# Adaptive layer norm block: the context of global attention is transposed by DMA instead of TensorE, and the last batch's norm is spread over twelve tiles

## Chip, cores and metric

One core of a Trainium2 chip. The metric is the device time of one launch in microseconds. The kernel before takes 2309.56 us in the median of 3 runs (2308.02 to 2310.95).

## What is computed

```python
mod = (silu(c) @ wmod).reshape(4, 6, 1, 256)             # sa, ca, ga, sb, cb, gb
h = layernorm(x) * (1 + ca) + sa                         # x: 4 batches, 1024 tokens, 256
q, k, v = (heads(tanh(h @ W + bias)) for W, bias in ...) # 16 heads of 64
ctx = softmax(causal(q @ k.T / 8)) @ v                   # global attention, each batch
x = x + ga * tanh(merge(ctx) @ Wo + bo)
h = layernorm(x) * (1 + cb) + sb
for l in range(2):                                       # local attention and gated feed-forward
    h = layer(h)
x = x + gb * h
```

Products are made in about full precision: each operand is split into a high part and a rest (low part), and three products are summed (high by high, high by low, low by high).

## The kernel before, in words

**Phase 1** (`phase_modulation_and_attention`, up to about 967 us of the trace) treats the 4 batches in order, and in each batch 8 pairs of heads. Each engine runs its own instruction list; semaphores order them. In a list written out by hand, a pair's work is interleaved with the projections (V, Q, K; six of 128x512, L777) of the next pair. The scores of a pair come in 12 units (`UNITS`): units 0 to 3 belong to the first half of the queries (c = 0, 512 tokens), units 4 to 11 to the second half (c = 1). Units 8 to 11 cross the diagonal and have 1024, 768, 512 and 256 elements. For a unit TensorE makes the scores into one of two PSUM tiles (`score_products`, L799; it needs the exponentials of two units before), ScalarE the exponentials (`exps`, L621), VectorE the high and low part (`high_probs`, `low_probs`, L359 and L365), and TensorE the products with the values (`value_products`, L821) into `ps_o`. Tokens are then on the partitions.

The **context** is a half's result. VectorE takes reciprocals of the sums (L373) and multiplies (`normalise`, L380) into the f32 tile `ctx_tok`, 128x512. For c = 0 this is done in the middle of the pair, for c = 1 at its end. But both halves are transposed at the end: `context` (L841) makes four TensorE transposes of 128x128 through `ctx_tok` for each half, before and after unit 0 of the next pair's scores. (With `ctx_tok` as one buffer and c = 1 written after L847 of c = 0, the first group's transposes read the half normalised in mid pair.) ScalarE copies the PSUM result into `cT_hi` (L641), VectorE subtracts it from PSUM into `cT_lo` (L386). Both are f32r, with head channels on the partitions, for all 8 pairs and 1024 tokens. At the end of a pair's VectorE list also stand the low part of the next weights (`split_weights`, L349), for which TensorE's next projections wait, and that of the last projection (L357).

At a **batch's end** TensorE makes the output projection (L957 to L967): for each half c and each 128 output columns m, 8 pairs by three products of 128x512 from `cT_hi` and `cT_lo`. ScalarE takes tanh (L742), VectorE multiplies by ga (`gate_attended`, L561), TensorE transposes back (`output_T`, L856), VectorE adds (L571). Other work is hung in between: for batches 0 and 1 the norm and transposed input of batch b + 2, for batches 2 and 3 the second norm of finished batches: `second_statistics`, `second_normal` on ScalarE (L666, 8 instructions a batch, after the first tanh), `second_scale` and `second_offset` on VectorE (L440, L446). For batch 3, ScalarE also copies the first layer's weights (L749) and VectorE takes their low part (L605). In these lists an instruction that waits holds back everything behind it.

SyncE's list issues the DMAs: weights of the pair after next (`load_w`, L234), the transposing DMAs for the values (`transpose_values`, L240 and L242; inputs are [64, 1024] and [128, 1024], two bytes an element), inputs and results of batches.

**Phase 2** (`phase_layers`) has two layers of 32 tiles of 128 tokens (local attention) and 8 chunks (feed-forward). Tiles are written out for the first four (`V_RING`) and the last ones, and looped between. The last batch's second norm is done in the first four tiles of layer 1: after tile 0 VectorE makes 8 statistics (L1514) and the variance, after tile 1 the shifts (L1522) while ScalarE makes 8 normalising instructions (L1494), after tile 2 VectorE scales (L1526), after tile 3 it adds the offset (L1531). At a layer's start GpSimd makes inverse norms of keys (L1210) and queries (L1206), and then adds the rotated halves of the queries and the keys (`add_rotated`, L1214), whose sum TensorE transposes (L1890).

## Time and profile before

| | us |
|---|---|
| median of 3 runs | 2309.56 |
| the profiled execution's own time | 2310.14 |
| span of the profile, first to last instruction | 2307.8 |
| first pair to end of global attention | about 57 to 967 |
| layers 1 and 2 | about 969 to 2308 |

The profile is one execution. A timeline line gives start, duration, engine, line and operation, the output tile before the arrow and its inputs behind it. Runs of equal instructions are merged (x4), and then start and duration hold for all of them. Durations of neighbours on one engine overlap by 0.03 to 0.4 us, since they are pipelined; the distance of starts is what an instruction costs its engine. Idle time stands in brackets with what ended it.

### The profile page before, as it was taken

The numbers are of one execution on the slowest core, as the hardware profiler recorded it, in microseconds if no ns is written. First come the engines' busy times: TensorE is split into PE (matmuls) and PEld (weight loads), VectorE is DVE, ScalarE is ACT, GpSimd is POOL, SyncE is SP. The second block draws the span as 40 slices with busy tenths as digits, with TensorE's granted clock in tenths as the row PEclk, the third lists the DMA queues.
The fourth block names the chain that finished last, engine by engine and source line by source line (L and its number), as shares of the span: only waits on it lengthen the run. The fifth ranks groups of instructions, "written<-read, shape, count | busy, mean of one in ns | idle before, by whom it ended". The sixth has DMA issues, their size and how long they took to land.

```text
span 2307.8 us, 60013 instructions
## 1 busy us (share of the span) xinstructions
PE 2219.3 (96%) x20608; PEld 1701.0 (74%) x20608; DVE 1900.7 (82%) x4480; ACT 1481.4 (64%) x2937; POOL 526.4 (23%) x637
## 2 busy tenths in 40 slices
PE   6999999999999999789999998999999999998999
PEld 4676767676767666667777776788777777776888
DVE  6999799979998999678888887567588888886776
ACT  5777577757776777366767766444567767765343
POOL 2000000000000000244554554012355555551000
PEclk9999999999999999999999999999999999999999
DMA  4311231113121212300000001000100000001110
GB/s 134 68 32 39 58 56 32 39 53 61 32 69 49 53 32 44 124 1 2 9 0 9 0 9 49 10 0 0 49 1 4 6 4 5 5 4 32 61 36 28
DMA packets 135595, 74.98 MB, mean 32 GB/s; under 512 B 72645, under 2 KB 132925, under 8 KB 135233
## 3 DMA queue, kind: packets, MB, share of 16 engines
q1 hardware_dynamic: 135488, 73.60, 13.0%
q8 instruction: 63, 1.03, 0.2%
q14 instruction: 44, 0.35, 0.1%
HBM read 44.21 MB, written 8.40 MB: 23 GB/s over the span
## 4 chain that ended last, share of the span: by engine, by line
PE 53%; DVE 2%; issue 1%; ACT 1%; POOL 0%; DVEq 0%; POOLq 0%; ACTq 0%
PE ly_ps L75 9%; PE ly_ps L76 9%; PE ly_ps L77 9%; PE ly_ps L1919 6%; PE ly_ps L1898 5%; PE ly_ps L1909 5%; PE ly_ps L1936 5%; PE ly_ps L1890 3%; PE ly_ps L1929 1%; PE ly_ps L1946 1%; PE ly_ps L1974 1%; PE ly_ps L1867 1%; DVE ly_masked L1587 1%; ACT ly_probs L1360 0%; DVE ly_rope_t L1558 0%
## 5 line engine op out<-in xcount | busy, mean ns | idle before, releaser
L625 ACT ACTIVATE at_p<-at_ps_s,at_shift 128x1024 f32<-128x1024 f32 (+3 forms) x384 | 335.9, 900 | 70.2 <-PE at_ps_s L817 39.0
L368 DVE TENSOR_TENSOR at_p_lo<-at_p,at_p_hi 128x1024 f16<-128x1024 f32 (+3 forms) x384 | 358.6, 954 | 5.5
L1360 ACT ACTIVATE ly_probs<-ly_masked,ly_small,ly_rq 128x256 f32<-128x256 f32 x512 | 301.7, 594 | 13.9 <-DVE ly_small L1590 13.9
L836 PEld LDWEIGHTS at_ps_o<-at_v,at_p_hi 128*128 128x128 f16 x2304 | 208.5, 97 | 58.2 <-issue 38.8
L836 PE MATMUL at_ps_o<-at_v,at_p_hi 128*128 128x65 f16 x2304 | 237.8, 195 | 6.0 <-DVE at_p_lo L368 3.1
L1214 POOL TENSOR_TENSOR ly_rope_a<-ly_rope_a,ly_rope_t 128x512 f32<-128x512 f32 x128 | 164.2, 1283 | 315.6 <-DVE ly_rope_t L1558 315.6
L837 PE MATMUL at_ps_o<-at_v,at_p_hi 128*128 128x64 f16 x2304 | 236.1, 193 | 0.0
L838 PE MATMUL at_ps_o<-at_v,at_p_lo 128*128 128x65 f16 x2304 | 234.9, 193 | 0.0
L1587 DVE CUSTOM_DVE_ANT_0 ly_masked<-ly_ps,ly_mask 128x256 f32<-128x256 f32 x512 | 195.8, 419 | 46.7 <-PE ly_ps L1898 35.7
L363 DVE CAST at_p_hi<-at_p 128x1024 f16<-128x1024 f32 (+3 forms) x384 | 206.4, 555 | 19.3 <-ACT at_p L625 15.4
L1368 ACT ACTIVATE ly_operands_plain<-ly_ps 128x512 f32<-128x512 f32 x256 | 153.2, 599 | 107.6 <-PE ly_ps L1909 99.7
L838 PEld LDWEIGHTS at_ps_o<-at_v,at_p_lo 128*128 128x128 f16 x2304 | 211.6, 98 | 0.0
L837 PEld LDWEIGHTS at_ps_o<-at_v,at_p_hi 128*128 128x128 f16 x2304 | 211.4, 99 | 0.0
L631 ACT ACTIVATE at_stage<-at_ps_m,at_bias 128x512 f32<-128x512 f32 x192 | 131.6, 686 | 104.0 <-PE at_ps_m L77 97.0
L75 PE MATMUL ly_ps<-ly_a_hi,ly_operands 128*128 128x512 f32 x384 | 169.4, 441 | 11.8 <-DVE ly_kn L1570 6.0
L75 PE MATMUL at_ps_m<-at_hT,at_w_hi 128*128 128x512 f32 (+1 forms) x384 | 169.0, 440 | 6.3 <-DVE at_hT L418 3.4
L1909 PE MATMUL ly_ps<-ident,ly_probs 128*128 128x128 f32 x1024 | 155.6, 275 | 6.1 <-ACT ly_operands_plain L1368 3.5
L1919 PE MATMUL ly_ps<-ly_operands_plain,ly_values 128*64 128x128 f32 x2048 | 155.6, 283 | 4.0 <-ACT ly_operands_plain L1368 4.0
L76 PE MATMUL ly_ps<-ly_a_lo,ly_operands 128*128 128x512 f32 x384 | 153.6, 400 | 0.0
L77 PE MATMUL ly_ps<-ly_a_hi,ly_operands 128*128 128x512 f32 x384 | 152.9, 398 | 0.0
L77 PE MATMUL at_ps_m<-at_hT,at_w_lo 128*128 128x512 f32 (+1 forms) x384 | 152.5, 397 | 0.0
L76 PE MATMUL at_ps_m<-at_hT,at_w_hi 128*128 128x512 f32 (+1 forms) x384 | 150.7, 392 | 0.0
(241 smaller groups left out, 5897.9 us busy)
## 6 DMA issues: line engine op xcount, KB each, us to landing
at_w_raw<-in_Wv SPq DMA_DIRECT2D x32, 128.0 KB, 2.2
at_w_raw<-in_Wq SPq DMA_DIRECT2D x32, 128.0 KB, 2.4
at_w_raw<-in_Wk SPq DMA_DIRECT2D x32, 128.0 KB, 2.4
at_xio<-in_states SPq DMA_DIRECT2D x4, 1024.0 KB, 5.7
ly_a_raw<-x SPq DMA_DIRECT2D x8, 512.0 KB, 3.9
out<-stream SPq DMA_DIRECT2D x16, 256.0 KB, 2.3
ly_shifted<-stream SPq DMA_DIRECT2D x8, 508.0 KB
x<-at_xio SPq DMA_DIRECT2D x3, 1024.0 KB, 4.4
```

Of the source, the lines that this page charges most:

```text
L75: pe.matmul(out, w_hi, x_hi, start=first, stop=False, skip_group_check=True)
L76: pe.matmul(out, w_hi, x_lo, start=False, stop=False, skip_group_check=True)
L77: return pe.matmul(out, w_lo, x_hi, start=False, stop=last, skip_group_check=True)
L368: dve.tensor_tensor(p_lo[u % P_RING][:, :, off:], probs[u % P_RING][:, :, off:], p_hi[u % P_RING][:, :, off:], ALU.subtract).then_inc(p_lo ...
L625: act.activation(probs[u % P_RING][:, :, off:], ps_s[u % 2][:, :, off:], ACT.Exp, bias=shift[:], scale=SCORE_SCALE).then_inc(exp_done, 1)
L836: pe.matmul(out, ph, ones_hi, start=(kt == 0 and t == 0), stop=False, skip_group_check=True)
L837: pe.matmul(out[:, 0:DH], ph, lo, start=False, stop=False, skip_group_check=True)
L838: step = pe.matmul(out, pl, ones_hi, start=False, stop=(kt == qc * CT + t), skip_group_check=True)
L1360: step = act.activation(pr[:, j % 2, h, :], sm[:, j % 2, h, :], ACT.Exp, bias=small[:, j % 2, 1, h:h + 1], scale=rq[:, par, 2 * j + h:2 * ...
L1587: dve.tensor_tensor_reduce(sm[:, j % 2, h, :], ps_s[h][:, half], mask[:, par].rearrange("p a b -> p (a b)"), 1.0, -3.0e38, ALU.add, ALU.ma ...
L1909: step = pe.transpose(ps_pt[:, (2 * slot + h) * P:(2 * slot + h + 1) * P], pr[:, j % 2, h, slot * P:(slot + 1) * P], ident[:])
L1919: step = pe.matmul(ps_pv[h * DH:(h + 1) * DH, j * P:(j + 1) * P], vv[:, v_slots[slot], cols], pT[:, j % 2, (2 * slot + h) * P:(2 * slot + ...
```

## The change

The context stays with tokens on the partitions while it is split. ScalarE makes an f16 high part `ctx_hi` from `ctx_tok`, in SBUF (for c = 0 between the exponentials of units 8 and 9, for c = 1 at the pair's end), VectorE the f16 low part `ctx_lo` (for c = 0 behind `high_probs` of unit 9). Two transposing DMAs of SyncE bring a half's parts into `cT`, now f16; SyncE waits for their landing and raises `ct_out`, which the next `high_context` needs. TensorE's `context` is gone. Before the output projection the f16 parts are copied into f32r (`cw`, for one half): ScalarE the high part, VectorE the low part, one pair at a time. So `second_normal` stands behind the second tanh. `y` now lies over `p_hi`. TensorE's waits on `ct_lo` in `project` (L768, L770) become waits on `pj_hi`, and the first `load_attended` of batch 3 in SyncE's list stands behind the context of pair 31's first half.

In layer 1 the last batch's norm is cut into four pieces of two token tiles and done in tiles 0 to 11, all written out: statistics behind tiles 0 to 3, variance behind 4, shifts behind 5, ScalarE's part behind 6 to 9, scales behind 7 to 10, offsets behind 8 to 11. At both layers' starts GpSimd's first `add_rotated` is put ahead of the inverse norms of the queries.

```diff
 rsum = a.sb("at_rsum", [P, 2, CT])
 with ExitStack() as shared:
-    cT = Allocator(nc, shared).sb("at_cT", [P, 2, HP, S], F32R)
+    over = Allocator(nc, shared)
+    cT = over.sb("at_cT", [P, 2, HP, S], F16)
+    cw = over.sb("at_cT_wide", [P, 2, HP, CH], F32R)
 first = a.sb("at_first", [P, 2 * HP * S])
-cT_hi, cT_lo = cT[:, 0], cT[:, 1]
+ctx_hi, ctx_lo = (a.sb(f"at_ctx_{part}", [P, CT, 2, DH], F16) for part in ("hi", "lo"))
...
+def transpose_context(it, c):
+
+    n = it * NC + c
+    cols = slice(c * CH, (c + 1) * CH)
+    sp.wait_ge(ct_hi, at(n + 1))
+    sp.wait_ge(ct_lo, at(n + 1))
+    for part, tokens in enumerate((ctx_hi, ctx_lo)):
+        sp.dma_start(cT[:, part, it % HP, cols].rearrange("p (t c) -> p t c", t=CT),
+                     tokens[:].rearrange("p t h d -> p (t h d)"), transpose=True).then_inc(ct_dma, 16)
+    sp.wait_ge(ct_dma, 32 * (n + 1))
+    sp.sem_inc(ct_out, 1)
+
...
-ahead = HP if b + 2 < B else HP - 1 if b + 1 < B else HP - 2
-for j in range(ahead):
-    n = b * HP + j + 2
-    sp.wait_ge(wh_done, at(n))
-    sp.wait_ge(wl_done, at(n))
-    load_w(n)
-    transpose_values(n - 1)
+for j in range(HP):
+    it = b * HP + j
+    if b + 2 == B and j + 1 == HP:
+        sp.wait_ge(pj_mm, at(NPJ * HP * (b + 1)))
+        for i in range(b):
+            load_attended(i)
+    if it + 2 < NPAIR:
+        sp.wait_ge(wh_done, at(it + 2))
+        sp.wait_ge(wl_done, at(it + 2))
+        load_w(it + 2)
+    if j:
+        transpose_context(it - 1, 1)
+    if it + 1 < NPAIR:
+        transpose_values(it + 1)
+    transpose_context(it, 0)
...
 def normalise(it, c):
     n = it * NC + c
     dve.wait_ge(r_done, at(n + 1))
-    if c == 1:
-        dve.wait_ge(ct_mm, n)
...
+def low_context(n):
     dve.wait_ge(ct_hi, at(n + 1))
-    cols = slice(c * CH, (c + 1) * CH)
-    dve.tensor_tensor(cT_lo[:, hp, cols], ps_m[c][:], f32(cT_hi[:, hp, cols]), ALU.subtract).then_inc(ct_lo, 1)
+    dve.tensor_tensor(ctx_lo[:], ctx_tok[:], ctx_hi[:], ALU.subtract).then_inc(ct_lo, 1)
+
+def wide_low(b, c, hp):
+    dve.wait_ge(ct_out, at((b * HP + hp) * NC + c + 1))
+    wide_free(dve, b, c, hp)
+    dve.tensor_copy(cw[:, 1, hp], cT[:, 1, hp, c * CH:(c + 1) * CH]).then_inc(cw_lo, 1)
...
 exps(it, 8)
+high_context(it * NC)
 exps(it, 9)
...
+def high_context(n):
+    hold(act, tick, (cx_done, at(n + 1)), (ct_out, at(n)))
+    act.activation(ctx_hi[:], ctx_tok[:], ACT.Copy).then_inc(ct_hi, 1)
+
+def wide_high(b, c, hp):
+    act.wait_ge(ct_out, at((b * HP + hp) * NC + c + 1))
+    wide_free(act, b, c, hp)
+    act.activation(cw[:, 0, hp], cT[:, 0, hp, c * CH:(c + 1) * CH], ACT.Copy).then_inc(cw_hi, 1)
...
 high_probs(it, 9)
+low_context(it * NC)
 high_probs(it, 10)
...
+for hp in range(HP):
+    wide_low(b, 0, hp)
+if b + 2 < B:
+    statistics(b + 2)
+else:
     second_statistics(0 if b + 1 < B else b - 1)
 if b + 2 == B:
     second_statistics(1)
     second_shifts(0)
 gate_attended(0, 0)
+for hp in range(HP // 2):
+    wide_low(b, 1, hp)
 if b + 2 < B:
-    statistics(b + 2)
-    gate_attended(0, 1)
     shifts(b + 2)
     normalise_chunk(b + 2, 0)
+    gate_attended(0, 1)
+elif b + 1 < B:
+    second_shifts(1)
+    gate_attended(0, 1)
+else:
+    second_shifts(b - 1)
+    gate_attended(0, 1)
+for hp in range(HP // 2, HP):
+    wide_low(b, 1, hp)
+if b + 2 < B:
     normalise_chunk(b + 2, 1)
     stream_lo(b + 2, 0)
     gate_attended(1, 0)
     add_attended(0)
     stream_lo(b + 2, 1)
 elif b + 1 < B:
-    second_shifts(1)
     second_scale(0)
     second_offset(0)
-    gate_attended(0, 1)
     second_scale(1)
     gate_attended(1, 0)
     add_attended(0)
     second_offset(1)
 else:
-    second_shifts(b - 1)
     second_scale(b - 1)
-    gate_attended(0, 1)
     second_offset(b - 1)
...
+for hp in range(HP):
+    wide_high(b, 0, hp)
 for c in range(NC):
     for m in range(KT):
+        if (c, m) == (0, 1):
+            for hp in range(HP // 2):
+                wide_high(b, 1, hp)
         act.wait_ge(op_mm, b * NC * KT + c * KT + m + 1)
         if m == 0:
             act.wait_ge(yt_mm, at(b * NC + c))
         act.activation(y[:, m, :], (ps_s[1], ps_o)[c][:, m, :], ACT.Tanh, bias=bo[:, m:m + 1]).then_inc(y_done, 1)
-        if m == 0 and c == 0 and b + 2 >= B:
-            second_normal(0 if b + 1 < B else b - 1)
-        if m == 1 and c == 0 and b + 2 == B:
-            second_normal(1)
-        if m == 1 and c == 0 and b + 1 == B:
-            act.wait_ge(keep["ld_a"], 16)
-            act.activation(a_hi[:], a_raw[:], ACT.Copy).then_inc(a_hi_done, 1)
-        if m == 1 and c == 0 and b + 2 < B:
-            stream_hi(b + 2, 0)
+        if (c, m) == (0, 1):
+            for hp in range(HP // 2, HP):
+                wide_high(b, 1, hp)
+            if b + 2 >= B:
+                second_normal(0 if b + 1 < B else b - 1)
+            if b + 2 == B:
+                second_normal(1)
+            if b + 1 == B:
+                act.wait_ge(keep["ld_a"], 16)
+                act.activation(a_hi[:], a_raw[:], ACT.Copy).then_inc(a_hi_done, 1)
+            if b + 2 < B:
+                stream_hi(b + 2, 0)
...
-context(it, 0, ahead_of)
 if ahead_of:
     scores(b, it + 1, 1 - par, 0)
-context(it, 1, ahead_of)
...
+if m == 0:
+    pe.wait_ge(cw_hi, (b * NC + c) * HP + hp + 1)
+    pe.wait_ge(cw_lo, (b * NC + c) * HP + hp + 1)
 step = three_products(pe, (ps_s[1], ps_o)[c][:, m, :], wo_hi[:, hp, outs], wo_lo[:, hp, outs],
-                      cT_hi[:, hp, c * CH:(c + 1) * CH], cT_lo[:, hp, c * CH:(c + 1) * CH],
-                      hp == 0, hp == HP - 1)
+                      cw[:, 0, hp], cw[:, 1, hp], hp == 0, hp == HP - 1)
+if m + 1 == KT and hp + 1 < HP:
+    step.then_inc(oc_mm, 1)
...
 inverse_key_norms(l, 0)
+add_rotated(l, 0, 0)
 inverse_query_norms(l, 0, 0, LP)
-add_rotated(l, 0, 0)
 add_rotated(l, 0, 1)
...
+head = HEAD if l == 0 else V_RING
+for t in range(head):
     tile(l, t, t % 2, (t + 1) % TB, t // 2, first=t == 0)
     if l == 0:
-        if t == 0:
-            last_statistics()
+        if t < NORM_PIECES:
+            last_statistics(t)
+        elif t == NORM_PIECES:
             last_variance()
-        elif t == 1:
+        elif t == NORM_PIECES + 1:
             last_shifts()
-        elif t == 2:
-            last_scale()
-        else:
-            last_offset()
+        elif NORM_PIECES + 2 < t < 2 * NORM_PIECES + 3:
+            last_scale(t - NORM_PIECES - 3)
+        if t > 2 * NORM_PIECES - 1:
+            last_offset(t - 2 * NORM_PIECES)
...
+if l == 0 and NORM_PIECES + 1 < t < 2 * NORM_PIECES + 2:
+    if t == NORM_PIECES + 2:
+        act.wait_ge(n0_col, 1)
+        act.wait_ge(keep["st_x1"], 16 * B)
+    for i in piece(t - NORM_PIECES - 2):
         step = act.activation(x[:, NT - TB + i, :], x[:, NT - TB + i, :], ACT.Identity,
                               scale=col0[:, 2, i:i + 1], bias=col0[:, 3, i:i + 1])
     step.then_inc(n0_xn, 1)
...
```

## Rows read from the trace of the kernel before

**Rows 1.** Busy time by stage: stretch, length, busy (x instructions), granted clock, DMA share, GB/s.
```profile
106.88:132.23 25.35, 25.11 (x350) 17.49 (x348) 24.20 (x38) 19.23 (x28) 0.00 (x0) 1.00 0.18 36
...
713.82:730.86 17.04, 17.03 (x72) 13.42 (x72) 13.24 (x36) 9.26 (x18) 3.52 (x2) 1.00 0.00 0
```

**Rows 2.** Timeline of TensorE at a pair's end: start, duration, operation.
```profile
121.55 0.63 PE L847 MATMUL at_ps_m<-ident,at_ctx_tok 128*128 128x128 f32 x4
...
122.11 0.39 PE L809 MATMUL at_ps_s<-at_q1hi,at_k1hi 64*128 64x512 f16 x2
```

**Rows 3.** Timeline of VectorE, same pair; in brackets idle time before, and its releaser.
```profile
114.70 0.69 DVE L363 CAST at_p_hi<-at_p 128x1024 f16<-128x1024 f32 x1 [0.45 <-ACT at_p L625]
...
117.18 0.89 DVE L363 CAST at_p_hi<-at_p 128x768 f16<-128x768 f32 x2
...
121.75 0.21 DVE L373 RECIPROCAL at_rsum<-at_ps_o 128x8 f32<-128x8 f32 x1 [0.16 <-PE at_ps_o L838]
...
122.22 0.69 DVE L380 TENSOR_TENSOR at_ctx_tok<-at_ps_o,at_rsum 128x512 f32<-128x512 f32 x1 [0.26 <-PE at_ps_m L847]
```

**Rows 4.** Timeline of ScalarE and TensorE in the same pair, around units 8 to 11.
```profile
113.56 1.91 ACT L625 ACTIVATE at_p<-at_ps_s,at_shift 128x1024 f32<-128x1024 f32 x2 [0.67 <-PE at_ps_s L817]
...
115.52 0.23 PE L809 MATMUL at_ps_s<-at_q0hi,at_k0hi 64*128 64x128 f16 x2
```

**Rows 5.** Groups of instructions by form, same pair: count, busy us, mean ns, idle before.
```profile
L363 DVE CAST at_p_hi<-at_p 128x512 f16<-128x512 f32 x2 | 0.8, 423 | 0.0
...
L641 ACT ACTIVATE at_cT<-at_ps_m 128x512 f32 x2 | 1.2, 595 | 0.6 <-PE at_ps_m L847 0.6
```

**Rows 6.** Timeline of SyncE's queue; then DMA issues (median us from issue to landing).
```profile
105.73 2.53 SPq L240 DMA_TRANSPOSE at_v<-at_vT_hi  x2
...
at_v<-at_vT_hi SPq DMA_TRANSPOSE x64, 2.8
...
at_v<-at_vT_lo SPq DMA_TRANSPOSE x32, 3.2
```

**Rows 7.** Timeline of TensorE, first output product of batches 2 and 3.
```profile
713.82 0.47 PE L75 MATMUL at_ps_s<-at_cT,at_wo_hi 128*128 128x512 f32 x1 [0.90 <-DVE at_cT L386]
...
938.92 0.47 PE L75 MATMUL at_ps_s<-at_cT,at_wo_hi 128*128 128x512 f32 x1
```

**Rows 8.** Timeline of ScalarE, VectorE and TensorE at the end of batch 2.
```profile
721.77 4.05 ACT L666 ACTIVATE stream<-stream,at_columns 128x256 f32<-128x256 f32 x8 [1.40 <-DVE at_columns L433]
...
725.93 2.29 DVE L440 TENSOR_TENSOR stream<-stream,modB 128x2048 f32<-128x2048 f32 x1 [2.10 <-ACT stream L666]
...
739.00 0.55 PE L856 MATMUL at_ps_o<-ident,at_y 128*128 128x128 f32 x3 [1.30 <-DVE at_y L563]
```

**Rows 9.** Timeline of ScalarE, VectorE and TensorE at the end of batch 3.
```profile
950.97 2.76 ACT L749 ACTIVATE ly_a_hi<-ly_a_raw 128x3072 fp32r<-128x3072 f32 x1
...
955.96 3.35 DVE L605 TENSOR_TENSOR ly_a_lo<-ly_a_raw,ly_a_hi 128x3072 fp32r<-128x3072 f32 x1
...
963.71 0.55 PE L856 MATMUL at_ps_o<-ident,at_y 128*128 128x128 f32 x3 [1.30 <-DVE at_y L563]
```

**Rows 10.** Timeline of TensorE: output projections of tiles 0, 3, 4 and 5 of layer 1.
```profile
1007.73 1.99 PE L1936 MATMUL ly_ps<-ly_operands_plain 128*128 128x256 f32 x8
...
1058.04 1.13 PE L1936 MATMUL ly_ps<-ly_operands_plain 128*128 128x256 f32 x4
...
1073.31 0.92 PE L1936 MATMUL ly_ps<-ly_operands_plain 128*128 128x256 f32 x3
...
1087.31 0.92 PE L1936 MATMUL ly_ps<-ly_operands_plain 128*128 128x256 f32 x3
```

**Rows 11.** Waits of TensorE, 964 to 1062 us; timelines of GpSimd and VectorE.
```profile
PE ly_ps L1890 <- POOL ly_rope_a L1214: 4.0, 1, 4.0
...
979.04 1.64 POOL L1206 TENSOR_TENSOR ly_rq<-ly_norm,ly_expo 128x8 f32<-128x8 f32 x1
...
979.14 0.74 DVE L1558 TENSOR_TENSOR ly_rope_t<-ly_ps,ly_rope 128x256 f32<-128x256 f32 x2
```

More of the change, by code:

```diff
@@ L989, with piece @@
 X1_RING = 3
+NORM_PIECES = 4
+HEAD = 3 * NORM_PIECES
+def piece(n):
+    return range(n * TB // NORM_PIECES, (n + 1) * TB // NORM_PIECES)
 def phase_layers(nc, io, scr, keep):
@@ L1309, in _ @@
                         carry_out(l, 2, 0, 2)
-                    for t in range(V_RING):
+                    head = HEAD if l == 0 else V_RING
+                    for t in range(head):
                         tile(l, t, t % 2, (t + 3) % TB)
-                        if l == 0 and t == 0:
+                        if l == 0 and t == NORM_PIECES:
                             pool.wait_ge(n0_var, 1)
@@ L1487, in _ @@
                 for l in range(L):
-                    for t in range(V_RING):
+                    head = HEAD if l == 0 else V_RING
+                    for t in range(head):
                         tile(l, t, t % 2, (t + 2) % V_RING)
-                        if l == 0 and t == 1:
-                            act.wait_ge(n0_col, 1)
-                            act.wait_ge(keep["st_x1"], 16 * B)
-                            for i in range(TB):
+                        if l == 0 and NORM_PIECES + 1 < t < 2 * NORM_PIECES + 2:
[3 more added lines that the diff above has]
+                            for i in piece(t - NORM_PIECES - 2):
                                 step = act.activation(x[:, NT - TB + i, :], x[:, NT - TB + i, :], ACT.Identity,
@@ L1496, in _ @@
                             step.then_inc(n0_xn, 1)
-                    with act.Fori(V_RING // 2, NT // 2 - 2) as i:
+                    with act.Fori(head // 2, NT // 2 - 2) as i:
                         for par in range(2):
@@ L1510, in _, with last_statistics @@
                 start(dve, DVE_SEMS)
[L1512 to L1513 removed]
+                def last_statistics(n):
+                    for t in piece(n):
                         dve.bn_stats(st0[:, t, :], x[:, NT - TB + t, :]).then_inc(n0_bn, 1)
```

88 lines of the change are left out of this document (39 added, 49 removed).

## The prediction

> **What bounds the kernel now.** I read the page's busy shares first: TensorE is busiest, VectorE next, and ScalarE has room. Such shares average over stages, so I asked for the busy time of one head pair. It lasts 25.35 us at full granted clock, with TensorE busy for 25.11 and VectorE for 24.20 [rows 1]. The reader should see that two engines are nearly full. Whatever is taken off TensorE is worth at most what VectorE, ScalarE and the order of the work let it use. Then I read the pair's timeline for VectorE's idle time. There is 0.45 us for exponentials, 0.16 for the last value product and 0.26 for the transposes that free the context tile, 0.87 in all [rows 3]. VectorE alone would need 25.35 - 0.87 = 24.48 us a pair. At the ends of batches 2 and 3 I read who waits in the chain tanh, gate, transpose back [rows 8, 9]. For the start of layer 1 I read the distances of the tiles [rows 10]. The sum stands against the profiled execution's 2310.14 us, which is 0.6 above the median.
>
> **Ordinary pair ends (28: seven a batch).** Removed are 2 of the 64 groups of four transposes. One group takes TensorE from 121.55 to 122.11, so 0.56 us, and two take 1.12 [rows 2]. The unit behind them still waits for its semaphore, so I take off 0.1.
>
> VectorE's subtraction and ScalarE's copy are of the same size as before, 128x512, now from SBUF. I cost them at no change. They are placed differently, though. ScalarE's high part of the first half now stands between the exponentials of units 8 and 9. These start at 113.56 and take 1.91 us together, and TensorE starts unit 11, which needs unit 9's, at 115.52, right at their end [rows 4]. The copy put between them costs ScalarE about 0.57 us (0.595 less overlap [rows 5]). Nothing covers it: TensorE's unit 11, and all queued behind it in its list (value products, two projections), moves back by 0.57. At the pair's end TensorE now reaches the next projections about as early as the low part of the weights is ready, which VectorE makes right behind its normalising [rows 3]. I put 0.05 for that. Left is 1.12 - 0.1 - 0.57 - 0.05 = 0.40 us, a pair of 24.95 us, above VectorE's 24.48. Times 28 this is **-11.2 us**. The bounds are 0 and VectorE's 0.87 a pair.
>
> **The transposing DMAs** are outside the sum as long as they land in time. `ct_out` must be up before ScalarE's `high_context` of the second half. VectorE's low part of the first half ends 0.6 us after unit 9's cast. From there VectorE has unit 10's cast, three low parts, a cast and two low parts of projections, the reciprocals and the normalising: from about 117.6 to 122.9, 5.3 us [rows 3]. Behind it stand the weights' low part and a projection's low part, before `low_context` wants the copy: some 0.85 us more. The cover is 6.1 us. Two issues take 2.53 us, and one transfer of 64x1024 lands 2.8 us after its issue began, one of twice the size after 3.2 [rows 6]. New is 128x512, as large as the first. So the round trip is 1.27 + 2.8 = 4.1 us, or 4.5 by the larger one, if they overlap as the values' do. If not, it is 5.6 to 6.4. SyncE waits for the landing, and queued behind it are the loads of weights and the values' transposes. These are wanted most of a pair later. I take 4.1, since size and kind agree.
>
> **Batch ends.** (a) TensorE's first product waited for the low part of the first half. Now VectorE must do a projection's low part, the second half's low part and one widening (0.42 by the f32 to f16 cast of that size [rows 5]; 0.68 if it runs as a subtraction does). That adds 0.6 + 0.42 and saves 0.26, so with rounding 0.7 us, for four batches. The rest of the first half's 16 copies keep ahead. An output triple takes TensorE 3 x 17.04/72 = 0.71 us [rows 1], a copy 0.42 or 0.6. (b) In the last pairs of batches 0 to 2 unit 11 is late as well, which makes 3 x 0.57 = 1.7. In the last pair, which VectorE bounds, its moved subtraction adds 0.6.
>
> (c) Batch 2. `second_normal` started at 721.77, behind the first tanh, and its 8 instructions fed the scale at 725.93 [rows 8]. Now it stands behind the second tanh and four widenings. First product 713.82 [rows 7] + 0.7, 48 products of 0.2366 (11.4), tanh 0.6, four copies 2.4 and the 8 instructions 4.0 give 732.9. VectorE's scale starts 7.1 us later than before. From the scale to the last gate it has 10.5 us of work (two scales and two offsets of 2.29 [rows 8], a gate, an addition) and had idled for 1.59 before that gate. So the gate is at 743.5 and the transposes back at 744.0 instead of 739.00: +5.0 with (a). TensorE has nothing else there.
>
> (d) Batch 3, likewise. First product 938.92 [rows 7] + 0.7 + 0.6, plus 11.4 + 0.6 + 2.4 + 4.0, is 958.6. The weights' copy (2.76) runs beside the scale and offset. VectorE needs 10.0 us with the weights' low part of 3.35, so the transposes back come at 969.2 instead of 963.71 [rows 9]: +5.5. What is late next is the start of the layers, by as much.
>
> Batch ends together: 0.7 x 2 + 5.0 + 5.5 + 1.7 = **+13.6 us**. The bounds are 3 us (all of (c) and (d) covered) and 17 (slow copies, which TensorE then waits for).
>
> **Layers.** From tile 0 to tile 4 there are 65.58 us, and one tile later 14.00 [rows 10]: the norm costs 65.58 - 56.0 = 9.6 us. The offset takes VectorE 2.29 as in batch 2 [rows 8], while the tile with it lasted 15.27, 1.27 more [rows 10], so a tile absorbs some 1.0 us. The pieces are 0.6 us, in three tiles two of them (1.2), ScalarE's 1.0. I leave 0.7 uncovered: -8.9. For the GpSimd swap, TensorE waited 4.0 us for the first addition, ahead of which stood 1.64 us of query norms. Its input, the rotated halves, is ready at 979.88, 0.84 us behind their start [rows 11], so I take 0.7 as gained in layer 1. In layer 2 another wait ends at the same place, nothing. Together **-9.6 us**. The bounds are 0 and -10.5.
>
> Sum: -11.2 + 13.6 - 9.6 = -7.2 us, 2302.9 against the profiled run, **2302.4** against the median.
>
> **Rivals.**
> A. VectorE alone sets the pair (24.48): TensorE's late unit 11 is caught up. 28 x 0.87 = -24.4, ends +11.9, layers -9.6: 2287.5. For it speaks that in-order engines with three buffers can slide. Against it, unit 11 started just when its exponential ended.
> B. The pair doesn't shorten, since VectorE at 95% busy can't gain against ScalarE's and TensorE's new order: +13.6 - 9.6 = +4.0, 2313.6.
> C, slower: the landing of the transposes becomes the wait. It stands at `high_context` of the second half on ScalarE, with the next pair's exponentials behind it. It decides from a round trip of 6.1 us; each further microsecond costs 28. At 6.9 us (transfers one after the other, 6.4, and 0.5 for the semaphores between) the pair ends give +11.2 in place of -11.2: 2324.8. The total turns to a loss at 6.4. Against it: the values' three transfers lie 1.27 us apart and still land in 2.8 to 3.2 [rows 6]. By the Trainium skill (VectorE: DVE Perf Modes, "The three transpose paths") a 128x128 block takes 1309 ns by DMA and 390 ns on TensorE, and TensorE is to be preferred. Eight blocks one after the other would be an estimated 10.5 us, 4.4 over the cover, some +116 us in all. By the trace eight blocks of the low values land in 3.2 us [rows 6], so the rule as a serial price does not hold here, and I give it no more than this rival's chance.
> D. The chain of (c) and (d) is covered: ends +5.1, 2293.9. The lists stand against it.
> E. The tiles' 9.6 us are not the norm's but code or cold buffers: only 0.7 is won, 2311.3. Against it: the tile with the offset alone has 1.27 us more, the next one none [rows 10].
>
> **Chances.** Forecast 0.45 (its own range 2296 to 2308), A 0.17, B 0.15, C 0.08, D 0.08, E 0.07. About 0.2% (4.6 us) can be told from no change. Faster: 0.36 of the forecast, A and D, 0.60. Same: the rest of the forecast, half of B, most of E, 0.23. Slower: half of B, C and slow ends, 0.17. The range takes in A's better part and B: 2286 to 2316. It leaves out C.
>
> **What would show it.** No L847. Pair distance 24.95 us (24.5 is A, 25.35 B, above it with ScalarE waiting on SyncE C). TensorE's unit 11 waits 0.6 us for exponentials. First output product 0.7 us later behind the last value product. The transposes back at the ends of batches 2 and 3 wait several microseconds for VectorE's gate, it for ScalarE's L666. Tiles 0 to 4 of layer 1 take 56 to 57 us. The prediction is wrong if the pair distance lies outside 24.7 to 25.2 or batches 2 and 3 lose under 7 us together.

## The result and the profile after

The median is 2316.68 us (2316.23 to 2321.37, six runs) against 2309.47 for the kernel before (six runs): 7.2 us slower, ratio 1.0037, interval 1.0025 to 1.0048. The forecast was 2302.4, the range ended at 2316. Both were missed, and the sign too. The profiled execution took 2320.11 us, 3.4 above the median; its span is 2318.3 against 2307.8. Four of the six executions lie at 2316.2 to 2316.7 us with a mean granted clock of 0.986 to 0.987 of full speed, the profiled one has 0.985, and the slowest, 2321.37, has 0.984. So the trace below shows somewhat more of the lower clock than the median does.

I cut both spans at the same instructions: VectorE's reciprocal of a pair's second half, TensorE's last transposes back (eight on `y`), and the layers' first transposes of `ly_xs`.

| stretch, us | before | after | change | forecast |
|---|---|---|---|---|
| to the first such reciprocal | 71.01 | 70.72 | -0.3 | 0 |
| 27 distances of ordinary pairs | 684.15 | 679.68 | -4.5 | -10.8 |
| end of batch 0, last reciprocal to the next | 53.76 | 56.29 | +2.5 | +1.3 |
| end of batch 1 | 53.77 | 57.85 | +4.1 | +1.3 |
| end of batch 2 | 52.17 | 60.72 | +8.6 | +5.6 |
| last pair | 22.04 | 23.81 | +1.8 | +0.2 |
| last reciprocal to the last transposes back | 26.81 | 33.40 | +6.6 | +4.9 |
| from there to the layers' first transposes | 5.09 | 5.01 | -0.1 | 0 |
| layers, from there to the end | 1339.03 | 1330.81 | -8.2 | -9.6 |
| sum | 2307.8 | 2318.3 | +10.5 | -7.2 |

So against this trace 17.7 us are missing (14.3 against the median): 6.3 in the pairs, 10.4 from the end of batch 0 to the last transposes back, 1.4 in the layers, less 0.4 in the two other stretches.

**The ordinary pair.** First the page's group of TensorE's first products of a projection, then the pair by the table of stretches (columns as in [rows 1]), then the timelines of ScalarE, TensorE and VectorE in the same pair of the changed kernel.

```profile
L75 PE MATMUL at_ps_m<-at_hT,at_w_hi 128*128 128x512 f32 (+1 forms) x384 | 169.5, 441 | 14.0 <-DVE at_w_lo L376 10.1
```
```profile
106.79:131.96 25.17, 24.03 (x342) 16.75 (x340) 24.05 (x38) 19.23 (x28) 0.00 (x0) 1.00 0.28 57
```
```profile
113.40 0.62 ACT L681 ACTIVATE at_ctx_hi<-at_ctx_tok 128x512 f16<-128x512 f32 x1
113.92 0.89 ACT L665 ACTIVATE at_p<-at_ps_s,at_shift 128x768 f32<-128x768 f32 x1
...
121.31 0.69 DVE L406 TENSOR_TENSOR at_ctx_tok<-at_ps_o,at_rsum 128x512 f32<-128x512 f32 x1
121.92 0.95 DVE L376 TENSOR_TENSOR at_w_lo<-at_w_raw,at_w_hi 128x768 fp32r<-128x768 f32 x1
...
123.31 0.50 PE L75 MATMUL at_ps_m<-at_hT,at_w_hi 128*128 x1 [0.50 <-DVE at_w_lo L376]
```

TensorE is busy for 24.03 us where it was 25.11 [rows 1]: the transposes are gone as forecast. The pair gives back only 0.18 of these 1.08 us. ScalarE's copy at 113.40 pushes the next exponential, as forecast. At the pair's end TensorE waits for the weights' low part, 26 times in the trace, 10.1 us in all; the forecast had 0.05 a pair for it. VectorE's subtraction begins only behind its normalising, at 121.92, and ends at 122.87; the projection starts 0.44 us behind that. The same two instructions in the kernel before (the next unit's last scores there start at 124.15):

```profile
122.83 0.95 DVE L349 TENSOR_TENSOR at_w_lo<-at_w_raw,at_w_hi 128x768 fp32r<-128x768 f32 x1
...
124.57 0.49 PE L75 MATMUL at_ps_m<-at_hT,at_w_hi 128*128 x1
```

From the unit's last scores to the projection there were 0.42 us, after the change there are 0.78 (122.53 to 123.31).

**The transfers** landed as forecast. SyncE's queue, then the group of those DMAs with its time to landing:

```profile
117.24 1.20 SPq L262 DMA_TRANSPOSE at_cT<-at_ctx_hi  x1
118.48 1.27 SPq L262 DMA_TRANSPOSE at_cT<-at_ctx_lo  x1
```
```profile
L262 SPq DMA_TRANSPOSE at_cT<-at_ctx_lo x64: 1252/1267/2235, 68.1 to 952.9; - x64
...
DMA to landing us min/median/max: 2.4/2.5/6.5
```

1.24 + 2.5 us are a round trip of 3.7, with the steps between about 4. Both are medians; the slowest landing is 6.5 us.

**Batch ends.** TensorE's first output product at the end of batch 0 in the timeline of after, then the stretch of the output products up to the last ones, before and after:

```profile
250.45 0.76 PE L75 MATMUL at_ps_s<-at_cT_wide,at_wo_hi 128*128 128x512 f32 x1 [2.55 <-DVE at_cT_wide L416]
251.01 0.63 PE L76 MATMUL at_ps_s<-at_cT_wide,at_wo_hi 128*128 128x512 f32 x1
```
```profile
251.20:265.45 14.25, 14.25 (x61) 11.20 (x61) 6.90 (x24) 1.38 (x2) 1.64 (x1) 1.00 0.00 1
```
```profile
250.45:266.25 15.80, 15.80 (x62) 12.67 (x63) 11.17 (x37) 8.37 (x15) 1.64 (x1) 0.89 0.19 41
```

The product comes 3.49 us behind the reciprocal instead of 2.78, the +0.7 of step (a). But TensorE now stands idle for 2.55 us (2.95 at batch 3), where before it had 0.90 [rows 7] with the context's transposes ahead of it. And its granted clock falls: the column of the clock shows 0.89 in place of 1.00, and the first products cost 0.43 to 0.56 us from start to start instead of 0.24, that is the lower level of 1.2 GHz for some 3.4 us. The same 60 products take 1.55 us more. No step of the forecast had this. From the first of the table's reciprocals to the last, the clock is at the lower level for 26 us in this trace and never in that of the kernel before; from there to the layers' first transposes for 11.1 us and 0.8.

Not all of that lies behind the new gap. In the last pair, where the change adds none, the clock fell twice in this trace and not at all in that of experiment 4. The second fall begins at 946.8, behind an idle stretch of 1.38 us and ahead of batch 3's gap (949.05 to 952.00), and lasts until 957.0. The last pair in after, then in experiment 4 (the column with 0.88 and 1.00 is the clock):

```profile
925.28:949.09 23.81, 18.11 (x304) 12.22 (x301) 20.20 (x32) 11.91 (x16) 0.00 (x0) 0.88 0.12 24
```
```profile
921.89:943.52 21.63, 16.22 (x305) 10.88 (x304) 20.20 (x31) 11.92 (x16) 0.00 (x0) 1.00 0.11 23
```

The end of batch 2 in the timelines of ScalarE, VectorE and TensorE, which answers to [rows 8]:

```profile
733.38 7.98 ACT L711 ACTIVATE stream<-stream,at_columns 128x256 f32<-128x256 f32 x16
...
737.52 2.29 DVE L470 TENSOR_TENSOR stream<-stream,modB 128x2048 f32<-128x2048 f32 x1 [4.25 <-ACT stream L711]
...
747.99 0.48 DVE L593 TENSOR_SCALAR at_y<-at_y,modT 128x512 f32<-128x512 f32 x1
...
748.52 1.97 PE L895 MATMUL at_ps_o<-ident,at_y 128*128 128x128 f32 x8 [5.78 <-DVE at_y L593]
```

The chain is that of step (c): the norm late on ScalarE, the scale behind it, the gate behind 10.5 us of VectorE's work. TensorE waits 5.78 us, and the eight transposes behind that gap take 1.97 us, where eight took 1.09 at batch 3: again the lower clock.

Batch 3, VectorE and GpSimd, with the last transposes back (answers to [rows 9]):

```profile
966.86 5.85 DVE L416 CAST at_cT_wide<-at_cT 128x512 fp32r<-128x512 f16 x4
972.63 2.28 DVE L470 TENSOR_TENSOR stream<-stream,modB 128x2048 f32<-128x2048 f32 x1
...
977.15 3.35 DVE L645 TENSOR_TENSOR ly_a_lo<-ly_a_raw,ly_a_hi 128x3072 fp32r<-128x3072 f32 x1
...
966.82 5.60 POOL L366 TENSOR_TENSOR ly_rope<-ly_rope,ly_rows 128x512 f32<-128x512 f32 x4 [5.68 <-DMA ly_rows<-in_qk_rows]
...
982.48 1.09 PE L895 MATMUL at_ps_o<-ident,at_y 128*128 128x128 f32 x8 [2.22 <-DVE at_y L593]
```

Four widening copies cost 1.46 us each beside GpSimd's multiplications, and elsewhere 0.36 from start to start (0.42 each in duration).

**Layers.** Output projections of tiles 0 and 4, and a line of TensorE's waits:

```profile
1026.62 1.99 PE L1996 MATMUL ly_ps<-ly_operands_plain 128*128 128x256 f32 x8
...
1082.67 1.99 PE L1996 MATMUL ly_ps<-ly_operands_plain 128*128 128x256 f32 x8
```
```profile
PE ly_ps L1950 <- POOL ly_rope_a L1265: 4.2, 3, 3.0
```

Tiles 0 to 4 take 56.05 us instead of 65.58 [rows 10]: the norm's 9.5 us are gone.

### The profile page after: what moved, and what is told of

It is laid out like the page before. It is cut to its first block, busy times and chain, and to the rows that moved or that the text cites. A ratio compares the mean times of both kernels' runs of the same rounds, so it can differ in the third digit from the quotient of the medians.

```text
span 2318.3 us, 59460 instructions
## 1 busy us (share of the span) xinstructions
PE 2199.8 (95%) x20352; PEld 1685.2 (73%) x20352; DVE 1922.9 (83%) x4550; ACT 1517.9 (65%) x3001; POOL 527.6 (23%) x637
## 4 chain that ended last, share of the span: by engine, by line
PE 54%; DVE 2%; issue 1%; ACT 1%; POOL 0%; DVEq 0%; POOLq 0%; ACTq 0%
PE ly_ps L75 9%; PE ly_ps L76 9%; PE ly_ps L77 9%; PE ly_ps L1979 6%; PE ly_ps L1958 6%; PE ly_ps L1969 5%; PE ly_ps L1996 5%; PE ly_ps L1950 3%; PE ly_ps L1989 1%; PE ly_ps L2006 1%; PE ly_ps L2034 1%; PE ly_ps L1927 1%; DVE ly_masked L1645 0%; DVE ly_operands_plain L1707 0%; ACT ly_probs L1412 0%
## 5 line engine op out<-in xcount | busy, mean ns | idle before, releaser
L75 PE MATMUL at_ps_m<-at_hT,at_w_hi 128*128 128x512 f32 (+1 forms) x384 | 169.5, 441 | 14.0 <-DVE at_w_lo L376 10.1
```

Source lines behind the costliest of these rows:

```text
L75: pe.matmul(out, w_hi, x_hi, start=first, stop=False, skip_group_check=True)
```

## Experiments

All are compared with the kernel before on the same chip. "Changed" is the kernel after.

**1. The two parts alone.** The kernel before with the layers' part:

> The kernel before, with only the second phase's part of the change (norm in four pieces over twelve tiles, GpSimd's first addition ahead of the query norms). Theory: this part brings what the prediction gave it, about 9 us (tiles 0 to 4 of layer 1 in 56 to 57 us instead of 65.6, 0.7 us at the start of layer 1): about 2300.5 us. Rival: in the changed kernel the layers' gain came from elsewhere, or is bought in other places by twelve written-out tiles: 2306 us or more.

Measured 2301.96 us (2300.94 to 2306.19), ratio 0.9965 [0.9952, 0.9977]. In the profile, tiles 0 to 4 take 56.05 us. Repeated later on another chip:

> The kernel before with the layers' part of the change alone, once more, beside the mended kernels on one chip. 2301 to 2303 us, ratio 0.9965.

Measured 2301.84, ratio 0.9967 [0.9954, 0.9979]. The attention part alone:

> The kernel before with the attention part of the change alone (context on token partitions, transposed by transfers, widened at a batch's end); the layers keep the norm over sixteen tiles. Theory, that the two parts add: after minus the 7.5 us that the layers' part gave by itself, so 2316.7 + 7.5 = 2324 us, 14.7 above the kernel before; ratio 1.0064. Of the profile: last reciprocal of the attention to the first output projection of the layers about 77 us as after, then about 1300 us as before. Rival, that the attention's end is late only because the layers' part shares something with it (the clock, GpSimd): below 2320.

Measured 2324.34 us (2323.87 to 2336.14), ratio 1.0067 [1.0050, 1.0084], +14.8 where +14.7 was expected. The two parts add: the layers' part is -7.3 us against the kernel before on its chip (-8.1 in the repeat), the attention's +14.8, together +7.5 where the whole change has +7.2. The rival (something shared) falls. The whole loss is in the attention.

**2. ScalarE's copy one unit later.**

```diff
                         exps(it, 8)
-                        high_context(it * NC)
                         exps(it, 9)
+                        high_context(it * NC)
```

> The changed kernel, with ScalarE's high part of the first half behind the exponentials of unit 9 instead of between those of units 8 and 9. Theory (order of the lists): TensorE's wait before unit 11 falls back from 0.87 to about 0.35 us, a pair gets 0.5 us shorter (25.17 to about 24.7), in all some 15 us: about 2302 us. Rival (VectorE full): VectorE's own 24.5 us plus its waits hold the pair near 25.1, the wait moves to the low part of the weights: 2314 us or more.

Measured 2308.18 us (2304.33 to 2311.45), ratio 0.9993 [0.9983, 1.0002]: 8.5 us better than after, but 6 less than expected. The pair in the table of stretches, and its copy:

```profile
106.17:131.05 24.88, 24.12 (x342) 16.74 (x340) 23.97 (x38) 19.28 (x28) 0.00 (x0) 1.00 0.29 58
```
```profile
111.92 1.90 ACT L665 ACTIVATE at_p<-at_ps_s,at_shift 128x1024 f32<-128x1024 f32 x2 [0.67 <-PE at_ps_s L866]
113.72 0.63 ACT L681 ACTIVATE at_ctx_hi<-at_ctx_tok 128x512 f16<-128x512 f32 x1
```
```profile
PE at_ps_m L75 <- DVE at_w_lo L376: 15.1, 27, 0.7
```

Most pairs are 24.75 to 24.9 us, 0.33 shorter than after (27 of them: 670.8 against 679.7). So the copy did cost the pair, by 0.33 of the 0.52 us it puts on unit 11. The rest went into the wait for the weights' low part, which grew from 10.1 to 15.1 us. That wait is what stands behind everything TensorE saves at the pair's end.

The same trace bears on the batch ends. TensorE is idle for 2.73 to 2.75 us before the first output products of batches 0 to 2, and the clock does not fall behind any of the three (1.00 in the stretches). The first output product of batch 0, then the stretch from it:

```profile
247.92 0.48 PE L75 MATMUL at_ps_s<-at_cT_wide,at_wo_hi 128*128 128x512 f32 x1 [2.73 <-DVE at_cT_wide L416]
```
```profile
247.92:263.00 15.08, 15.08 (x69) 12.31 (x70) 11.99 (x40) 8.38 (x15) 1.64 (x1) 1.00 0.25 50
```

This execution has 0.988 as its mean clock, and seven of the other nine have 0.984 to 0.986 and are 2.5 to 7.1 us longer. So its three clean batch ends are not the rule for this kernel.

**3. The weights' low part first.**

```diff
-                        reciprocals(it, 1)
-                        normalise(it, 1)
                         if ahead_of > 1:
                             split_weights(it + 2)
+                        reciprocals(it, 1)
+                        normalise(it, 1)
```

> The changed kernel, with VectorE's low part of the weights ahead of the reciprocals and the normalising of the second half. Theory: TensorE's wait before the next pair's first projection (0.72 us in the trace of the change, 0.36 before) goes back to 0.36, 0.35 us a pair, some 10 us: about 2306.5 us. Rival: the normalising, and with it the next pair's exponentials, come 0.9 us later and cost as much: 2315 us or more.

Measured 2331.28 us (2329.68 to 2333.21), ratio 1.0089 [1.0073, 1.0106]; the pair became 25.54. My theory missed, its rival came true. ScalarE at the pair's end, then TensorE's waits:

```profile
123.60 0.63 ACT L681 ACTIVATE at_ctx_hi<-at_ctx_tok 128x512 f16<-128x512 f32 x1 [0.83 <-DVE at_ctx_tok L406]
124.14 1.10 ACT L665 ACTIVATE at_p<-at_ps_s,at_shift 128x1024 f32<-128x1024 f32 x1
```
```profile
PE at_ps_s L858 <- ACT at_p L665: 37.2, 88, 1.6
```

The wait for the weights is gone, but the normalising ends 1.4 us later by this timeline, 0.7 of which is this run's shift. ScalarE waits for it with the next pair's exponentials queued behind the copy, and TensorE's waits for exponentials rise from 21.2 to 37.2 us. So the pair has two chains out of VectorE's last microseconds, and neither order serves both.

**4. TensorE kept busy in the gap.** Ten matmuls whose result nobody reads, ahead of the output products of each batch:

```diff
                     pe.wait_ge(wo_done, 2)
+                    for _ in range(10):
+                        pe.matmul(ps_s[1][:, 0, :], wo_hi[:, 0, 0:P], ...
```

> The changed kernel with ten idle products of 128x512 on TensorE, into a PSUM tile that is overwritten, in the 2.55 us before each batch's first output product. Theory: the granted clock halves at each batch's end (3.4 us and more at half) because TensorE now stands idle there; with the gap filled it stays full, the output products take 14.2 us for 60 again instead of 15.8, and some 8 us come back: about 2309 us. Rival (the clock falls for another reason, such as the load before): the clock still halves at the batch ends and the time is 2316 us or, with late products, more.

Measured 2314.00 us (2310.38 to 2316.28), ratio 1.0016 [1.0006, 1.0025]: 2.7 us better than after, 8 were expected. The end of batch 0 by stretch, then the first output product of batch 3:

```profile
252.00:270.00 18.00, 18.00 (x85) 14.64 (x85) 12.17 (x40) 10.96 (x19) 1.83 (x1) 1.00 0.16 31
```
```profile
946.54 0.47 PE L75 MATMUL at_ps_s<-at_cT_wide,at_wo_hi 128*128 128x512 f32 x1 [0.68 <-DVE at_cT_wide L416]
```

The clock stays at 1.00 (2.4 GHz). The ends of batches 0 to 2 take 54.78, 55.07 and 60.19 us instead of 56.29, 57.85 and 60.72, the last pair 21.63 instead of 23.81, and the tail to the last transposes back 32.22 instead of 33.40: 8.2 us in all. The last pair's 2.2 of these are not the idle matmuls' doing, since batch 3's stand behind it, and in the tail of after the clock had fallen before the gap. That leaves 4.8 us for batches 0 to 2 and up to 1.2 for the tail. This profiled execution also had the lower clock at other places (near the start and in the layers, where nothing was changed), and stretches outside the attention cost 4.4 us more than in the profile of after.

That the median shows still less has a reason in the other traces: a gap without the idle matmuls doesn't always bring the clock down. In seven traces without them (after, attention_alone, weights_first, norm_last, rope_later, normal_early, copy_behind_unit9) there are 21 gaps of 2.55 to 2.75 us at the ends of batches 0 to 2, and the clock fell at 14: three times in each of the first three, twice in norm_last and rope_later, once in normal_early, never in copy_behind_unit9. In the three traces with them (this one and the two mended kernels) it fell at none of nine. Where it happened not to fall in a kernel without them, the batch end is as short as here: batch 0 takes 54.75 us in norm_last and normal_early, batch 1 55.05 in rope_later. So the idle matmuls do keep the clock up there, and what they bring in an execution hangs on where the clock would have fallen in it.

**5. ScalarE's norm earlier**, at the ends of batches 2 and 3.

```diff
                                 for hp in range(HP // 2):
                                     wide_high(b, 1, hp)
+                                if b + 2 >= B:
+                                    second_normal(0 if b + 1 < B else b - 1)
...
                                     wide_high(b, 1, hp)
-                                if b + 2 >= B:
-                                    second_normal(0 if b + 1 < B else b - 1)
```

> The changed kernel with ScalarE's second norm (eight tiles of it) put ahead of the last four widening copies at the ends of batches 2 and 3. Theory, that the 5.8 us before TensorE's second transposes back at the end of batch 2 are the chain widening, second norm, scale, offset on VectorE: the scale can start 2.2 us earlier, and that gap goes from 5.8 to about 3.6 us; at batch 3 the a_hi copy follows as well and 1 to 2 us go. Together 3 to 4 us: about 2313 us. Rival, that VectorE's own widening and gates set it: under 0.7 us in all, 2316 to 2317 us.

Measured 2315.19 us (2313.22 to 2319.32), ratio 1.0029 [1.0019, 1.0039]: 1.5 us better than after, 3 to 4 were expected. ScalarE at the end of batch 2, and the gap:

```profile
723.67 4.04 ACT L711 ACTIVATE stream<-stream,at_columns 128x256 f32<-128x256 f32 x8
...
741.05 1.09 PE L895 MATMUL at_ps_o<-ident,at_y 128*128 128x128 f32 x8 [2.27 <-DVE at_y L593]
```

The gap went from 5.78 to 2.27 us (3.6 were expected), and the end of batch 2 from 60.72 to 54.87, of which 1.7 us are that no low clock followed the gap (2.27 us of idle time; in three_mended it did fall behind 2.28 us). At batch 3 the same move lost 1.4 us: the first tanh waits behind the norm, and TensorE behind it. So step (c) was a real chain, and the order there is a matter of each batch.

**6. GpSimd's multiplications held back** until the last widening copy is done.

```diff
+                pool.wait_ge(cw_lo, NC * NPAIR)
                 pool.wait_ge(keep["ld_rope"], 32)
```

> The changed kernel with GpSimd's four rope multiplications held until VectorE's last widening copy is done. Theory: VectorE's widening copies of 1.46 us beside them (0.36 to 0.48 elsewhere) are slow because both engines work on their operands in SBUF at once, so all four take under 0.5 us each and TensorE's three waits of 0.49 us in the output products of batch 3 go. The time moves little, since ScalarE's norm ends at 972.5 us all the same and VectorE's scale follows it: 0 to 1.5 us faster, 2315 to 2317 us. Rival, that the copies are slow for another reason (the DMA of the rope tables, TensorE's low clock): they still take over 1 us each.

Measured 2320.25 us (2319.11 to 2321.51), ratio 1.0047 [1.0030, 1.0063]. VectorE and GpSimd:

```profile
966.26 1.43 DVE L417 CAST at_cT_wide<-at_cT 128x512 fp32r<-128x512 f16 x4
971.95 3.02 DVE L471 TENSOR_TENSOR stream<-stream,modB 128x2048 f32<-128x2048 f32 x1 [4.25 <-ACT stream L712]
```
```profile
967.77 5.04 POOL L367 TENSOR_TENSOR ly_rope<-ly_rope,ly_rows 128x512 f32<-128x512 f32 x4 [7.48 <-DVE at_cT_wide L417]
```

The copies are back at 0.36 us each, so GpSimd's work beside them was the cause. Instead VectorE's scale, which begins while GpSimd still works, takes 3.02 us and not 2.29. As expected nothing is won, since the scale waits for ScalarE's norm in any case. The median is 3.6 us above after's, outside the expected range, for which I have no cause; the end of batch 2 in this profile is 62.51 us, 1.8 more, with no edit there, and the clock is low for 6.8 us there instead of 3.4.

**7. The transfers' cover.** Each pair of transposes issued twice, the second behind the landing of the first.

```diff
-                    for part, tokens in enumerate((ctx_hi, ctx_lo)):
-                        ...
-                    sp.wait_ge(ct_dma, 32 * (n + 1))
+                    for turn in range(2):
+                        for part, tokens in enumerate((ctx_hi, ctx_lo)):
+                            ...
+                        sp.wait_ge(ct_dma, 64 * n + 32 * (turn + 1))
```

> The changed kernel with every pair of context transposes issued twice, the second after the first has landed. The round trip goes from 4.0 to about 7.7 us, while from VectorE's low part at 117.2 us to ScalarE's next use of the buffers at 122.15 us there are 5.0 us. Theory, that the transfers are hidden with about 1 us to spare in the ordinary pair: ScalarE waits some 2.7 us at each pair's end and the pair grows by 2 to 2.7 us, to 27.2 to 27.9 us; the whole by 65 to 85 us, 2380 to 2400 us. Rival, that there is slack behind ScalarE that takes it up: the pair grows by under 0.5 us, under 2335 us.

Measured 2414.51 us (2406.65 to 2415.15), ratio 1.0457 [1.0440, 1.0475], above the expected 2400; most pairs are 27.55 us, as expected, and some 28 to 29.6. SyncE's queue, ScalarE at the pair's end, and ScalarE's waits:

```profile
149.80 1.19 SPq L263 DMA_TRANSPOSE at_cT<-at_ctx_hi  x1
...
153.57 1.19 SPq L263 DMA_TRANSPOSE at_cT<-at_ctx_hi  x1
154.80 1.27 SPq L263 DMA_TRANSPOSE at_cT<-at_ctx_lo  x1
```
```profile
157.46 0.63 ACT L682 ACTIVATE at_ctx_hi<-at_ctx_tok 128x512 f16<-128x512 f32 x1 [2.84 <-SPq L266]
```
```profile
ACT at_ctx_hi L682 <- SPq L266: 100.4, 32, 8.4
```

From 149.72, VectorE's low part, to 157.46 are 7.7 us for two round trips, and ScalarE waits 2.84. So the cover of one is 4.9 us, not the 6.1 of the prediction, and the changed kernel needs about 4 of it. Rival C was nearer than it looked.

**8. Batch 3's norm last**, on ScalarE behind the last tanh, scale and offset behind the last sum.

```diff
-                        second_scale(b - 1)
-                        second_offset(b - 1)
+                        gate_attended(1, 0)
+                        add_attended(0)
                         dve.wait_ge(a_hi_done, 1)
                         dve.tensor_tensor(a_lo[:], ...
-                        gate_attended(1, 0)
-                        add_attended(0)
                     gate_attended(1, 1)
                     add_attended(1)
+                    if b + 1 == B:
+                        second_scale(b - 1)
+                        second_offset(b - 1)
```

> The changed kernel with only that: batch 3's second norm behind the last tanh, scale and offset behind the last sum. Theory as before: 33.4 us from the last reciprocal to the last transposes back become 28 to 30, and the whole 2312 to 2314 us, of 2316.7. Rival, that the norm is covered and TensorE's own low clock sets this end: still 33 us, 2316 to 2318 us.

Measured 2317.50 us (2316.40 to 2326.30), ratio 1.0043 [1.0027, 1.0059]: no gain. TensorE, then VectorE:

```profile
978.71 1.09 PE L898 MATMUL at_ps_o<-ident,at_y 128*128 128x128 f32 x8 [1.30 <-DVE at_y L593]
988.79 1.08 PE L1930 MATMUL ly_ps<-ident,ly_xs 128*128 128x128 f32 x4 [8.99 <-POOLq L1240]
```
```profile
982.16 2.29 DVE L470 TENSOR_TENSOR stream<-stream,modB 128x2048 f32<-128x2048 f32 x1 [1.10 <-ACT stream L712]
984.49 2.29 DVE L476 TENSOR_TENSOR stream<-stream,modB 128x2048 f32<-128x2048 f32 x1
```

The last transposes back come 31.42 us behind the reciprocal instead of 33.40, but the layers start 10.08 behind them instead of 5.01: scale and offset now stand between. That is the rival as written for the combined run in experiment 9; the one written here (still 33 us) fell.

**9. The mends together**: experiment 2, 4, and 5 for batch 2 alone. Then the same with 8 on top.

> The changed kernel with three mends: the copy behind unit 9, ten idle matmuls in the gap before the output products, and the second norm of batch 2 ahead of the last four widening copies. Theory, that the loss is the sum of the late copy, the low clock and the chain of batch 2, each by itself: 2316.7 less 8.5 (copy), less 2.7 (idle matmuls, some of it twice counted), less 5 (batch 2 went from 60.7 to 54.9 us with the norm earlier; about 4 beside the others) gives about 2301 us, faster than the kernel before and about equal to the layers' part alone. Rival, that the falls of the clock move to other places and take it back: 2306 us or more.

> The three mends, and batch 3's second norm of the ninth to twelfth tiles put behind the last tanh on ScalarE and its scale and offset behind the last sum on VectorE. Theory, that this norm stands ahead of the last gate (VectorE's scale, offset and low half of the layers' weights, 7.9 us, begin only when ScalarE's norm ends): from the last reciprocal to the last transposes back 33 us become 28 to 29, and 3 us or so of it are kept behind: about 2297.5 us. Rival, that VectorE's scale and offset then delay the layers' first products by as much: 2301 us. If it holds, this beats the layers' part alone by some 4 us.

Measured 2298.03 us (2295.39 to 2299.78), ratio 0.9947 [0.9933, 0.9960], 3 better than expected; and 2293.71 (2293.35 to 2297.97), ratio 0.9934 [0.9921, 0.9948]. The intervals overlap, and in the profiles the second is ahead by 3.9 us already at the last reciprocal, before 8 touches anything; there the first has two more falls of the clock, one behind batch 2's gap and one in the last pair. From that reciprocal to the end both take 1365 us (1364.8 and 1365.0). So I count 8 as nothing, and its mechanism as not shown. Against the layers' part alone on the same chip (2301.84) the mended kernels are 3.8 and 8.1 us faster; the interval of the first mended kernel just overlaps that of the layers' part, but each of its five executions is shorter than all six of the layers' part. How much of the lead is the attention's own is not shown. Up to the layers' first transposes the profiles are ahead by 1.0 and 4.6 us; the other 4.3 lie in the layers, whose code is the same, with the clock low for 16 us there instead of 27. The kernel with norm_last has 16 too, those of after and copy_behind_unit9 have 27. By stretches in the profile of the first, against the kernel before: pairs 671.2 (-13.0), batch ends 54.43, 54.74, 56.03 (+5.5), last pair 23.44 (+1.4), tail 31.95 (+5.1): the attention is about even with the kernel before.

## Why the prediction was wrong

**Right.** Two groups of transposes gone, 1.08 us of TensorE's time a pair for 1.12. Unit 11 later by 0.52 for 0.57. VectorE's and ScalarE's durations for the split (0.68 and 0.63) as costed. The landing in 2.5 us in the median, rival C's condition not met. The first output product 0.7 us later at batches 0 to 2 (0.9 at batch 3). The chains (c) and (d): at full clock (experiment 4) the last transposes back came 32.77 us behind the reciprocal at batch 2 and 32.22 at batch 3, +4.8 and +5.4 for the forecast's +5.0 and +4.9. Rival D is refuted. The layers' norm 9.5 for 9.6, which refutes rival E. The GpSimd swap: in the two runs of the layers' part alone tile 0 comes 38.1 and 38.3 us behind the layers' first transposes instead of 38.9, which is 0.6 to 0.8 for the forecast's 0.7. The two tests that the text named for being wrong did not fire: the pair's mean of 25.17 is just inside 24.7 to 25.2, and batches 2 and 3 lost more than 7 us. They were too wide: from 24.95 to 25.17 alone are 6 us over the kernel, and a loss far above the forecast was not asked for.

**Wrong, first step: "I put 0.05 for that"**, the wait for the weights' low part at the pair's end. It was 0.36 more than before in a pair. The prediction shows no row for VectorE's subtraction, only the normalising ahead of it. By the trace of before it ends at 123.78, or 123.5 without the 0.26 us of waiting that the change takes away, and TensorE's projection at 124.57 moves to 123.45 with the two groups of transposes gone: it arrives before the subtraction has ended, and the trace of after adds 0.44 us from that end to the projection. What TensorE saves at the pair's end lands on that wait. Of the 1.08 us of work that are gone, 0.52 (the copy) and 0.36 (this wait) leave 0.20; measured are 0.17 a pair in place of 0.40, 6.3 us over 27 distances. Experiments 2 and 3 show it from both sides. Rival B was near the truth for the pair, though it gave as a reason VectorE's load and not that one wait.

**Wrong, second step: TensorE's rate at the batch ends**, "3 x 17.04/72 = 0.71" a triple, taken from a stretch at full clock. The change takes TensorE's last work there (the transposes) and makes its idle time 2.55 us; the clock was at the lower level for a while at the first output products of all four batches of the profiled execution. Between the trace of after and that of experiment 4 lie 8.2 us in these stretches, and 1.7 more lie behind batch 2's gap, about 10 against the 10.4 missing there. Shown as the gap's own are 4.8 us at batches 0 to 2 and at most 1.2 at batch 3; the last pair's 2.2 are falls of the clock that come and go without an edit there. In the median the gap is worth less (2.7 us by experiment 4), since the clock falls behind it in two cases of three.

**Small.** The cover of the transfers was 4.9, not 6.1. The prediction itself says that ScalarE's `high_context` must wait for `ct_out`, which follows the normalising at once, and yet adds 0.85 us of VectorE's work ahead of `low_context`. In the layers the GpSimd swap took the longest wait from 4.0 [rows 11] to 3.0 us, but in this trace the way from the layers' first transposes to tile 0 is 39.1 us against 38.9, with the clock low for 1.0 us more, which hides the swap's 0.7. The tiles 8 to 11 cost 0.5 us more, as far as allowed for. Behind tile 16 the layers take 0.6 us more (1067.0 against 1066.4), again with 1 us more of the low clock. That accounts for the layers' 1.4. The same layers' code takes 1064.3 us there with the clock low for 5 us and 1070.4 with 22 (norm_last and experiment 4). Why the clock falls at one place in one execution and not in another stays open.

## What to carry to other kernels

When a change frees an engine at one place, find the next semaphore that it runs into there and compare with the **end** of the instruction that raises it; two queues that leave one engine's last microsecond can't both be served first. When it takes TensorE's last work ahead of a wait, price the idle time at the clock too. A few matmuls that nobody reads can be cheaper than the gap. One profile can't tell what the clock costs: look at the same gap in several. And keep a change's parts apart: here one part won 7.3 us and the other lost 14.8, which the sum hid.

## What the runs showed of the hardware

- TensorE's granted clock went to 1.2 GHz behind idle stretches of 2.55 us and 5.78 us, and in the last pair behind 1.38 us, and stayed there for 3.4 to 10 us. Behind gaps of 2.55 to 2.75 us at one and the same place it fell 14 times of 21; with ten matmuls in them (up to 0.68 us idle left) none of nine times. Behind 0.90 us, in the kernel before, it had not fallen [rows 7].
- The time at the lower clock makes the spread between traces of equal code: the layers of the change take 1326.9 us with 16 us of it, 1331.3 with 27 and 1332.9 with 32 (norm_last, copy_behind_unit9, filled_gap).
- VectorE's copy f16 to f32r inside SBUF (0.36 to 0.42 us for 128x512) took 1.46 us beside GpSimd's multiplication, which itself takes 1.26 to 1.40: the copy lasts as long as GpSimd's instruction. The Trainium skill (SBUF — State Buffer, "Who interferes with whom") has VectorE and GpSimd share a port pair, which VectorE needs in some of its modes and for two inputs in SBUF, and which the first to issue holds for its whole instruction. The traces agree: the copies last as long as the multiplications beside them, and are back at 0.36 us when these are held back. The scale, too, with two inputs in SBUF, took 3.02 instead of 2.29 us.
- Two transposing DMAs of 128x512 f16 inside SBUF land in about 4 us from the first issue in the median (64 such pairs; 2.4 to 6.5 us a transfer from its own issue), while VectorE and TensorE work.
